# Mixture-of-experts stage of a graph kernel: second layer's bias moved from TensorE to ScalarE and VectorE, TensorE's loop written out

## What is computed

```
tokens = layernorm(x)
probs  = softmax(tokens @ router_w.T);  rw, re = top_k(probs, 2);  rw = rw / sum(rw)
out = tokens
for e in range(8):
    h = gelu(tokens @ w1[e] + b1[e])
    y = h @ w2[e] + b2[e]
    out = out + combine[:, e] * y          # zero except for the two chosen experts
x = x + out
```

## Time and profile before

| | |
|---|---|
| median of three runs | 1038.2 us |
| the profiled execution | 1039.9 us |
| its span, first to last instruction | 1037.8 us |
| TensorE busy | 885.1 us (85%) |
| VectorE busy | 800.8 us (77%) |
| ScalarE busy | 582.6 us (56%) |
| GpSimd busy | 461.9 us (45%) |
| granted TensorE clock, mean of the span | 0.899 |

### The profile page before, as it was taken

The page is one execution under the profiler, slowest core; times in us unless marked ns, Lnnn a source line. Parts: engine busy times, 40 slices in busy tenths (PEclk is TensorE's granted clock), DMA queues, the critical chain, the costliest instruction groups (busy, mean ns, idle before and its releaser), DMA issues.

```text
span 1037.8 us, 28856 instructions
## 1 busy us (share of the span) xinstructions
PE 885.1 (85%) x9598; PEld 812.9 (78%) x9599; DVE 800.8 (77%) x1801; ACT 582.6 (56%) x1565; POOL 461.9 (45%) x529
## 2 busy tenths in 40 slices
PE   0488888888887999649898746999999999999997
PEld 0477777777786899549898625999999999999996
DVE  6999999999958887656786894767776677767775
ACT  2345555555545766346556344666666666666664
POOL 9000000000037667577774003666666666666663
PEclk9889999999998999855555578999999999999999
DMA  6960000000025665456665191222222222222230
GB/s 202 294 226 21 30 20 30 20 30 20 31 84 172 199 189 157 122 150 206 202 207 177 38 7 48 84 76 78 78 79 75 74 75 82 84 77 81 74 67 10
DMA packets 78990, 103.26 MB, mean 99 GB/s; under 512 B 22505, under 2 KB 64482, under 8 KB 78938
## 3 DMA queue, kind: packets, MB, share of 16 engines
q0 software_dynamic: 21408, 54.87, 19.0%
q1 hardware_dynamic: 57530, 47.73, 16.5%
HBM read 62.12 MB, written 44.02 MB: 102 GB/s over the span
## 4 chain that ended last, share of the span: by engine, by line
PE 60%; DVE 25%; issue 6%; POOL 4%; DMA 2%; ACT 1%; DVEq 1%; POOLq 0%; ACTq 0%
PE bank L929 17%; PE bank L944 16%; DVE arena L1041 8%; PE bank L748 7%; PE bank L771 6%; DVE arena L1028 6%; POOL arena L504 3%; PE bank L829 3%; PE bank L895 3%; PE bank L939 3%; PE bank L783 2%; PE bank L792 2%; PE bank L840 2%; DMA arena<-src_cols 1%; DVE arena L1048 1%
## 5 line engine op out<-in xcount | busy, mean ns | idle before, releaser
L492 POOL DMA_INDIRECT arena<-key_rows,cid x98 | 93.4, 953 | 308.7 <-DVEq L1136 271.7
L720 ACT ACTIVATE arena<-bank,b1s 128x128 f32<-128x128 f32 x500 | 142.7, 368 | 124.0 <-PE bank L929 123.8
L944 PE MATMUL bank<-w2s,arena 128*128 x1500 | 197.8, 273 | 0.0
L929 PE MATMUL bank<-arena,w1s 128*128 128x128 f16 x3000 | 190.1, 220 | 5.5 <-issue 5.4
L929 PEld LDWEIGHTS bank<-arena,w1s 128*128 x3000 | 178.6, 99 | 10.8 <-issue 7.9
L519 POOL DMA_INDIRECT out<-arena,gidx x125 | 127.0, 1016 | 118.8 <-DVE arena L1339 100.5
L508 POOL DMA_INDIRECT arena<-tok_rows,gidx x125 | 121.7, 974 | 104.2 <-DVE gidx L1315 66.4
L944 PEld LDWEIGHTS bank<-w2s,arena 128*128 128x128 f16 x1500 | 146.8, 98 | 15.6
L748 PE MATMUL bank<-arena 125*128 125x100 bf16 x1600 | 83.8, 215 | 75.3 <-DVE arena L1041 75.3
L748 PEld LDWEIGHTS bank<-arena 125*128 125x128 bf16 x1600 | 80.1, 102 | 83.9 <-DVE arena L1041 47.3
L1336 DVE SCALAR_TENSOR_TENSOR arena<-bank,arena 128x256 f32<-128x256 f32 x125 | 60.5, 484 | 108.5 <-PE bank L944 108.2
(11 more groups left out here) (215 smaller groups left out, 1438.4 us busy)
## 6 DMA issues: line engine op xcount, KB each, us to landing
agg_rows<-arena SPq DMA_DIRECT2D x49, 256.0 KB, 2.5
tok_rows<-arena SPq DMA_DIRECT2D x13, 896.0 KB, 5.0
big<-x SPq DMA_DIRECT2D x6, 1792.0 KB, 15.1
arena<-w SPq DMA_DIRECT2D x16, 256.0 KB, 3.6
arena<-tok_rows,gidx POOLq DMA_INDIRECT x125, 2.8
out<-arena,gidx POOLq DMA_INDIRECT x125, 2.5
big<-x SPq DMA_DIRECT2D x1, 1664.0 KB
arena<-key_rows,cid POOLq DMA_INDIRECT x98
```

What stands on the lines that cost most here:

```text
L720: last = sc.activation(h32[:, u % 2, at:at + P], bank[2 + u % 2][:, at:at + P], ACT.Gelu, bias=b1s[:, ds(e[x], 1), f], scale=1.0 / SCALE)
L929: last = mm(bank[2 + u % 2][:, at:at + P], parts[x, w, c, f], a[:, u % 4, c * P:(c + 1) * P], start=(n == 0), stop=(n == 5))
L944: last = mm(to, a[:, u % 4, at:at + P], parts[x, w, c], start=False, stop=(n == 5))
```

## The change

Four things change. TensorE no longer adds the second layer's bias: the ones3 matmuls and the f16 rows of b2 are gone. In their place b2 is broadcast to all 128 partitions in f32 (b2t, one transfer of 1 MB after the aggregates are stored), and ScalarE scales it by 64 ahead of the third piece of the layer norm. In each step ScalarE writes mean + weight1 * b2[expert 1] into ob (first_bias, before gelu), and VectorE adds weight2 * b2[expert 2] (second_bias) and the scaled row (residual), for tile j, two steps before the tile's y is ready; VectorE therefore loads the table of experts too. The two additions of y stay, with the residual of another tile between them. ob has eight buffers and not four, so that out_stored counts per buffer of eight. And `schedule` writes out all steps of TensorE, without a loop.

```diff
@@ -199,9 +197,7 @@
 
         pg = two.take([P, 2, B, D], f32)
         tT = two.take([P, 2, 2 * D], f32)
-        b2r = two.take([P, E, D], f16)
-        b2p = two.take([E, 3, D], f16)
-        b2f = two.take([E, D], f32)
+        b2t = two.take([P, E, D], f32)
 
         three = Arena(big, T * D * 4)
         lgc, ohc = (three.take([P, RG, E], f32) for _ in range(2))
@@ -311,20 +307,21 @@
 
         def schedule(eng, step):
             known = {}
+            if eng is nc.tensor:
+                for j in range(-2, NT + 2):
+                    load_experts(eng, known, 0, j)
+                    step(j // DEPTH, j % DEPTH, j, known)
+                return
             for j in range(-2, DEPTH):
                 load_experts(eng, known, 0, j)
                 step(j // DEPTH, j % DEPTH, j, known)
             last = (NT - 2) // DEPTH
             with eng.Fori(1, last) as i:
                 known = {}
-                if eng is nc.tensor:
-                    known[-1] = word(eng, i * (DEPTH // AHEAD) - 1)
                 for u in range(DEPTH):
                     load_experts(eng, known, i, u)
                     step(i, u, None, known)
             known = {}
-            if eng is nc.tensor:
-                known[last * DEPTH // AHEAD - 1] = word(eng, last * DEPTH // AHEAD - 1)
             for j in range(last * DEPTH, NT + 2):
                 load_experts(eng, known, 0, j)
                 step(j // DEPTH, j % DEPTH, j, known)
@@ -334,7 +331,7 @@
 
         def load_experts(eng, known, i, u):
             k = u // AHEAD
-            if eng is not nc.vector and u % AHEAD == 0 and u < NT:
+            if u % AHEAD == 0 and u < NT:
                 known[k] = word(eng, i * (DEPTH // AHEAD) + k)
 
         def experts_of(known, u):
@@ -405,14 +402,10 @@
 
             sp.wait_ge(w_prep, 2 * E)
             sp.wait_ge(cid_ready, 1)
-            sp.dma_start(b2f, b2).then_inc(s_b2f, 16)
-            sp.wait_ge(b2p_ready, 1)
             sp.wait_ge(agg_stored[0], 16 * (T // 4 + 1))
             sp.wait_ge(agg_stored[1], 16 * (T // 4))
-            sp.dma_start(b2_rows.rearrange("n e d -> e n d"), b2p).then_inc(b2_split, 16)
-            sp.wait_ge(b2_split, 16)
-            sp.wait_ge(b2r_zeroed, 1)
-            sp.dma_start(b2r[0:3, :, :].rearrange("n e d -> n (e d)"), b2_rows.rearrange("n e d -> n (e d)")).then_inc(s_b2r, 16)
+            sp.dma_start(b2t.rearrange("p e d -> p (e d)"),
+                         b2.rearrange("(a e) d -> a (e d)", a=1).broadcast_to([P, E * D])).then_inc(s_b2, 16)
 
             for n, (first, more) in enumerate(PIECES):
                 sp.wait_ge(t_ready, first + more)
@@ -420,8 +413,8 @@
                              t32[:, n % 2, 0:more, :]).then_inc(rows_stored[n % 2], 16)
             sp.wait_ge(meta_ready, 1)
             sp.dma_start(tok_rows[:, D:ROW].rearrange("(t p) m -> p t m", p=P), meta[:, :, :]).then_inc(meta_stored, 16)
-            for k in range(4):
-                sp.wait_ge(out_stored[k], 16 * len(range(k, NT, 4)))
+            for k in range(DEPTH):
+                sp.wait_ge(out_stored[k], 16 * len(range(k, NT, DEPTH)))
 
 
         @block.gpsimd
@@ -516,8 +508,8 @@
                 gather_tile(j)
             for j in range(NT):
                 pool.wait_ge(o_ready, j + 1)
-                gp.indirect_dma_start(out, bass.IndirectOffsetOnAxis(gidx[:, j:j + 1], 0), ob[:, j % 4, :], None,
-                                      bounds_check=N - 1, oob_is_err=False).then_inc(out_stored[j % 4], 16)
+                gp.indirect_dma_start(out, bass.IndirectOffsetOnAxis(gidx[:, j:j + 1], 0), ob[:, j % DEPTH, :], None,
+                                      bounds_check=N - 1, oob_is_err=False).then_inc(out_stored[j % DEPTH], 16)
                 if j + DEPTH < NT:
                     gather_tile(j + DEPTH)
 
@@ -671,6 +663,10 @@
 
             m = 0
             for n, (first, more) in enumerate(PIECES):
+                if n == 2:
+                    act.wait_ge(s_b2, 16)
+                    flat = b2t.rearrange("p e d -> p (e d)")
+                    sc.activation(flat, flat, ACT.Copy, scale=SCALE).then_inc(b2_scaled, 1)
                 act.wait_ge(var_ready, T // 2 - PA + n + 1)
                 sc.activation(std[:, first:first + more], mv[:, first:first + more, 1], ACT.Sqrt,
                               bias=eps[:, :]).then_inc(std_ready, 1)
@@ -721,13 +718,21 @@
                                              bias=b1s[:, ds(e[x], 1), f], scale=1.0 / SCALE)
                 last.then_inc(gelu_ready, 1)
 
+            def first_bias(i, u, e):
+                if not isinstance(i, int) or i > 0:
+                    act.wait_ge(out_stored[u], 16 * i)
+                sc.activation(ob[:, u, :], b2t[:, ds(e[0], 1), :].rearrange("p a d -> p (a d)"), ACT.Identity,
+                              bias=xg[:, u, D + 1:D + 2], scale=xg[:, u, D + 2:D + 3]).then_inc(bias_ready, 1)
+
             def act_step(i, u, j, known):
                 if j is None or 0 <= j - 1 < NT:
                     high_hidden(*tile(i, u, -1))
                 if j is None or j + 2 < NT:
                     high_tokens(*tile(i, u, 2))
                 if j is None or 0 <= j < NT:
-                    gelu(i, u, experts_of(known, u if j is None else j))
+                    e = experts_of(known, u if j is None else j)
+                    first_bias(i, u, e)
+                    gelu(i, u, e)
 
             schedule(act, act_step)
 
@@ -936,12 +938,11 @@
                 wait_tile(pe, o_ready, i, u, -1)
                 for x in range(2):
                     to = bank[4 + u % 2][:, x * D:(x + 1) * D]
-                    mm(to, ones3[:, :], parts[x], start=True, stop=False)
                     n = 0
                     for c in range(2):
                         for a, w in ((hh, 0), (hl, 0), (hh, 1)):
                             at = (2 * x + c) * P
-                            last = mm(to, a[:, u % 4, at:at + P], parts[x, w, c], start=False, stop=(n == 5))
+                            last = mm(to, a[:, u % 4, at:at + P], parts[x, w, c], start=(n == 0), stop=(n == 5))
                             n += 1
                 last.then_inc(y_ready, 1)
 
@@ -1154,17 +1155,6 @@
                 ve.tensor_tensor(gat[:, of], wmi, wabs, ALU.add).then_inc(gat_ready, 1)
                 for d in steps_left[2 * b + 2:2 * b + 4]:
                     node_step(d)
-
-            dve.wait_ge(s_b2f, 16)
-            step(ve.tensor_scalar(b2f, b2f, SCALE, None, ALU.mult))
-            for n in range(3):
-                step(ve.tensor_copy(b2p[:, n, :], b2f))
-                if n < 2:
-                    step(ve.tensor_tensor(b2f, b2f, b2p[:, n, :], ALU.subtract))
-            dve.sem_inc(b2p_ready, 1)
-            dve.wait_ge(agg_stored[0], 16 * (T // 4 + 1))
-            dve.wait_ge(agg_stored[1], 16 * (T // 4))
-            ve.memset(b2r.rearrange("p e d -> p (e d)").bitcast(f32), 0.0).then_inc(b2r_zeroed, 1)
 
             def route(c):
                 first, n = ROUTED[c]
@@ -1325,25 +1315,42 @@
                 wait_tile(dve, y_ready, i, u, -3)
                 ve.tensor_tensor(hl[:, u % 4, :], h32[:, u % 2, :], hh[:, u % 4, :], ALU.subtract).then_inc(hl_ready, 1)
 
-            def result(i, u):
-                k = u % 4
-                if not isinstance(i, int) or 2 * i + u // 4 > 0:
-                    dve.wait_ge(out_stored[k], 32 * i + u // 4 * 16)
-                ve.tensor_scalar(ob[:, k, :], xg[:, u, 0:D], xg[:, u, D:D + 1], xg[:, u, D + 1:D + 2], ALU.mult, ALU.add
-                                 ).then_inc(res_ready, 1)
+            def second_bias(i, u, e):
+                wait_tile(dve, bias_ready, i, u, 1)
+                ve.scalar_tensor_tensor(ob[:, u, :], b2t[:, ds(e[1], 1), :].rearrange("p a d -> p (a d)"),
+                                        xg[:, u, D + 3:D + 4], ob[:, u, :], ALU.mult, ALU.add).then_inc(biases_ready, 1)
+
+            def residual(i, u):
+                wait_tile(dve, biases_ready, i, u, 1)
+                ve.scalar_tensor_tensor(ob[:, u, :], xg[:, u, 0:D], xg[:, u, D:D + 1], ob[:, u, :], ALU.mult, ALU.add
+                                        ).then_inc(res_ready, 1)
+
+            def first_expert(i, u):
                 wait_tile(dve, y_ready, i, u, 1)
                 wait_tile(dve, res_ready, i, u, 1)
-                ve.scalar_tensor_tensor(ob[:, k, :], bank[4 + u % 2][:, 0:D], xg[:, u, D + 2:D + 3], ob[:, k, :],
+                ve.scalar_tensor_tensor(ob[:, u, :], bank[4 + u % 2][:, 0:D], xg[:, u, D + 2:D + 3], ob[:, u, :],
                                         ALU.mult, ALU.add).then_inc(oa_ready, 1)
+
+            def second_expert(i, u):
                 wait_tile(dve, oa_ready, i, u, 1)
-                ve.scalar_tensor_tensor(ob[:, k, :], bank[4 + u % 2][:, D:2 * D], xg[:, u, D + 3:D + 4], ob[:, k, :],
+                ve.scalar_tensor_tensor(ob[:, u, :], bank[4 + u % 2][:, D:2 * D], xg[:, u, D + 3:D + 4], ob[:, u, :],
```

(14 more changed lines are left out.)

21 lines of the change are left out of this document (8 added, 13 removed).

## The result

| | before | after |
|---|---|---|
| median of four runs | 1038.2 us (1038.0 to 1040.2) | 1012.0 us (1010.9 to 1013.5) |
| the profiled execution | 1039.9 us | 1013.5 us |
| its span | 1037.8 us | 1011.5 us |

The ratio is 0.9742 [0.9728, 0.9755]: 26.2 us less, where the prediction had 34.8 less and 1003.4 us. The profiled execution, at 1013.5, is 8.4 us over its own forecast of 1005.1. The time lies inside the range, at its very upper end, where the prediction had put rivals 1 and 3. Neither turns out to be the cause, so that the range holds is luck.

The account below looks back on a forecast made before the run. TensorE was taken to bound the expert stage, everybody waiting for it. Fewer bias matmuls (27.3 us) and no loop turns (7.5) made 34.8 us less: 1003.4 us for the median, range 1000 to 1012.

Parts of the forecast that it names:

- Rival 1: Expert stage: VectorE's instructions run end to end, 2.93 us a step, 7.5 us given back, 1010.9 us; chance 4%.
- Rival 3: Expert stage: ScalarE's and VectorE's loop turns or table loads stop TensorE; only 27.3 us won, 1010.9 us; chance 7%.
- loop written out, bias on TensorE: TensorE's expert-stage loop: writing it out removes the holes at its turns, 7.5 us; bounds 0 and 7.5.
- bias moved, loop kept: TensorE's second layer: two matmuls fewer a tile at 0.109 us each, 125 tiles, 27.3 us.
- The step of TensorE: Expert stage: start to start of TensorE's transposes falls from 3.09 to 2.87 us, TensorE still the bound.
- rival 4: Expert stage: TensorE's written-out code arrives too slowly, a 0.55 us hole every tile, 69 us, 1072 us; chance 4%.
- VectorE: VectorE's additions in the expert stage: 2.42 us of a 2.87 us step, new instructions 0.35 each, bounds 0.33 and 0.53.
- Rival 2: Expert stage: VectorE paces, four combining instructions at 0.53 us each, 3.04 a step, 21 us back, 1024.7 us; chance 8%.
- The cover: VectorE's wait for ScalarE's first bias: slack of some 0.4 us; once gone, each 0.1 us past 2.87 costs 12.5 us.
- GpSimd and the transfers: Expert stage: GpSimd's store and gather take 2.62 us, staying under the 2.87 us step by a quarter of a microsecond.
- GpSimd's stores waiting for nothing but issue: Expert stage: one of the listed trace signs that would show the forecast wrong; no size given.

Follow-up runs that it names:

- written_out_2: Kernel before with only TensorE's expert-stage steps written out, bias matmuls kept, on another chip: 1032.0 us, ratio 0.9932.
- bias_moved_loop_2: Kernel after with TensorE's loop put back, bias still on ScalarE and VectorE: 1017.7 us, ratio 0.9798.
- after_again: Kernel after, unchanged, measured again beside later variants: 1012.6 us, ratio 0.9746 to the kernel before.
- twelve_buffers: Kernel after with twelve buffers instead of eight for gathered rows and output rows, ob moved elsewhere in SBUF: 1005.6 us, ratio 0.9676.
- adds_through_psum_2: Kernel after with the partial sum in PSUM, so residual and second bias read one SBUF tensor each: 1010.7 us; first run, slow chip, 1229.9.
- no_second_bias_2: Kernel after with both bias instructions left out and the old residual, b2 missing from the output: 1009.4 us, ratio 0.9715.
- second and third set: Follow-up runs made after a first group near 1235 us; the kernel before took 1039.3 us and 1039.8 us beside them.
- psum_twelve: Kernel after with both partial sums in PSUM and twelve buffers instead of eight: 1006.1 us, ratio 0.9678.

## Why the prediction was right in its range and 8.6 us low in its value

| term | forecast | measured |
|---|---|---|
| loop written out, bias on TensorE | 7.5 | 7.3 (written_out_2) |
| bias moved, loop kept | 27.3 | 21.6 (bias_moved_loop_2) |
| both | 34.8 | 27.2 (after_again), 26.2 (first comparison) |
| both, twelve buffers | | 34.2 (twelve_buffers) |

The forecast of the median was 8.6 us too low. The range was wide enough only because rivals 1 and 3 had been taken in, and both are false.

**The step of TensorE** was right: 2.87 us, and with twelve buffers the whole 34.8 us come out but for 0.6. A spacing read between two starts was the right price of a matmul. The written-out program cost nothing, against rival 4: the kernel after has 64 packets on queue q8 in the whole run where there were 28, written_out_2 has 66, and there no step after the sixth tile is over 3.13 us.

**VectorE** was 0.09 us over its value by starts (2.51 a step) because the new instructions follow at 0.40, inside the bounds of 0.33 and 0.53. Rival 1 is out: instructions of 0.48 us follow at 0.40. The prediction took for it one half of what the Trainium skill says (page VectorE: DVE Perf Modes, section The DRAIN you can't avoid). The same paragraph adds that a next op that isn't held starts earlier, and with that the 0.40 agree. Rival 2's 0.53 each is out as well. The cover held in the steady steps. It didn't hold in the first steps of the stage: there VectorE waits twice for ScalarE's first bias (0.43 us before 640.90, 0.42 before 643.35), and TensorE loses 0.9 us in the two steps after 642.30.

**Rival 3** gave the measured time within 1 us, 1010.9, for the wrong reason. In the kernel after VectorE's turns show as 0.15 to 0.21 us called issue before low_hidden, and TensorE's steps around those at 682.80, 776.87 and 871.02 are 2.87. Only small excesses (0.17 to 0.30 us, in the steps from 797.86, 823.98 and 917.82) lie near other turns, and so do the second and third cluster (turns at 846.45 and 963.10), but not the first. twelve_buffers, whose loops turn too though less often, has none.

**GpSimd and the transfers** is the step that failed. It was costed at nothing: "so GpSimd stays under it, by a quarter of a microsecond". It took the 2.62 us of the earlier trace rows for GpSimd's step whatever VectorE does, and asked only whether the mean fits, not what the quarter is needed for. The trace of before had two things to see. GpSimd is delayed by 1.07 us every 21 tiles, in a step of 4.16 us, and is back in time after two steps with 0.49 us of slack each; at 0.26 it needs four. And its instructions grow beside VectorE's. In the expert stage of before none does, but in the layer norm stage gathers do beside the additions of two SBUF tensors (L1209, from 445.75), and not beside the statistics that follow. Timeline of GpSimd, before:

```profile
447.97 1.04 POOL L504 DMA_INDIRECT arena<-agg_rows,gat  x1 [0.30 <-issue]
449.31 0.94 POOL L504 DMA_INDIRECT arena<-agg_rows,gat  x1 [0.30 <-issue]
```

In the kernel after the residual makes most gathers 1.17 us (2.87 a step, no slack at all). While GpSimd is late, low_hidden holds it first, and then the residual. With twelve buffers 7.0 us of the missing time come back. What part is due to what is only known in outline. With one input of each new instruction in PSUM (adds_through_psum_2) the time is still 1010.7: their two SBUF inputs are worth some 2 us or nothing, by the intervals, since low_hidden, unchanged, does the same at a step of 2.87. With no bias at all 3.2 us of the steps' loss are left, which is the part of the shorter step alone. The rest, 3.4 to 5.1 us by these single traces, goes with the added work of ScalarE and VectorE.

The prediction had named the right sign among those that would show it wrong, "GpSimd's stores waiting for nothing but issue"; it gave it no price.

Whether a delayed gather is held depends on where it falls. At a step of 3.09 it starts 0.09 us ahead of low_hidden (723.95 against 724.04) and goes free; at 2.87 it starts 0.11 behind. That the shorter step is enough to put GpSimd in the lock is shown by no_second_bias_2, which has neither bias instruction and the old residual.

**Open.** What GpSimd's delay of about 1.05 us is. It comes in every version, and always at the same tiles: the stores of tiles 24, 45, 66, 87 and 108 in the kernel before and in written_out_2, of 24, 65 and 106 in the second and third set's versions with eight output buffers (the stores of these tiles start late, marked issue, in adds_through_psum too, whose stage ran over 100 us later), of 22, 55 and 88 with twelve. So it goes by the place in GpSimd's program and not by the time. In the kernel before no packet of queue q8 is recorded from 679 to 1014 us, and of the three of the other instruction queue, q14, in that stretch none is at a delay of this size. Putting GpSimd's stores and gathers into a loop, which would have asked its program, wasn't tried. Why a second hole follows a wait in front of the transposes isn't settled either. And the scattered long steps marked issue (3.55 at 765.63) went with twelve buffers, but of most of them nothing ties them to a late gather.

The best version run that computes everything is twelve_buffers, 1005.6 us (ratio 0.9676); psum_twelve can't be told from it.

## What to carry to other kernels

When the bound engine gets faster, look at each engine that feeds it for its worst stretch and not its mean step: a lag that was made good within two steps may stay, as here, and then more tiles of lead can bring the time back. Read the slack as what pays for the rare delays, and ask how long after one the engine is back. A length taken from one neighbourhood of instructions isn't the engine's own where another engine can hold it; compare lengths of one instruction by what runs beside it.

## What the runs showed of the hardware

In these traces an indirect DMA instruction of GpSimd that starts while a VectorE instruction with two SBUF inputs is in work, at least 0.09 us after that one began, is longer by the rest of that instruction less 0.13 us: 1.17, 1.24, 1.28, 1.38 and 1.43 us for rests of 0.31, 0.39, 0.39, 0.54 and 0.57 (the gather alone takes 0.98, the store 1.02). With a rest of 0.13 or less it isn't longer. If it starts 0.08 us ahead of the VectorE instruction, it isn't held. With one input in PSUM (L1329 of adds_through_psum_2, in the same place beside the gather) it is 0.98, and with one SBUF input too. The Trainium skill, page SBUF — State Buffer, section SBUF: two separate sides, has VectorE and GpSimd share a pair of ports as an exclusive lock: of a VectorE instruction with two SBUF inputs and a GpSimd instruction that reads SBUF, the one that starts first has the pair for its whole length, and the other is blocked. The traces agree for one side only. GpSimd is held, but VectorE isn't: low_hidden is 0.68 us in each of its 111 instances from 650 to 1000 us of the kernel before, also at 724.04, where a gather had begun 0.09 ahead of it, and 0.68 or 0.69 in the kernel after. By that rule the new residual could have been seen to press on GpSimd, and the prediction didn't draw on it.

GpSimd, held in this way, fell into step with VectorE. Free to run at 2.61 us a step, it ran at TensorE's 2.87 for as long as it was late.

A wait of TensorE in front of its transposes came with a second hole. In the seven traces of the changed kernel and its variants that have such waits after 638 us, from 0.23 to 0.79 us, a hole of 0.53 to 0.75 us before the first layer follows each.
